# Experts' loop with rounds of 16 pairs on TensorE and of eight on ScalarE, expert words loaded within the steps, and sixteen staging buffers for normalised blocks

## What is computed

```python
scores = sigmoid(x @ gate_w.T);  sc = scores + gate_bias
group_scores = top_k(sc.reshape(T, 8, 8), 2)[0].sum(-1)     # 4 of 8 groups stay
tidx = top_k(masked, 8)[1]
tw = take_along_axis(scores, tidx) / sum * 2.5
y[t] = sum over the 8 experts e of tw * (silu(x We_gate[e]) * (x We_up[e])) We_down[e]
     + (silu(x Ws_gate) * (x Ws_up)) Ws_down
```

## Time and profile before

| | us |
|---|---|
| runs | median 1569.08 (1569.03 to 1569.74, three runs) |
| the profiled execution | 1555.25 |
| its span | 1553.5 |
| TensorE busy in the span | 1330.9 (86%) |
| VectorE busy | 933.4 (60%) |
| ScalarE busy | 850.4 (55%) |
| POOL busy | 626.7 (40%) |

### The profile page before, as it was taken

How to read it: one execution, slowest core, us unless ns; L and a number is a source line. 1 busy time by engine, 2 the same in 40 slices (tenths; PEclk the granted TensorE clock), 3 DMA queues, 4 the chain that set the end, 5 groups by cost and what they waited for, 6 DMA issues and landing times.

```text
span 1553.5 us, 38499 instructions
## 1 busy us (share of the span) xinstructions
PE 1330.9 (86%) x9262; PEld 1181.9 (76%) x9263; DVE 933.4 (60%) x4527; ACT 850.4 (55%) x2382; POOL 626.7 (40%) x750
## 2 busy tenths in 40 slices
PE   5873878788787897988888898988899789999996
PEld 5863767677666786877777777777787789999995
DVE  6771434334334453666666565665644589888997
ACT  2442565565555585554545454454555467777774
POOL 7026555556555500555555555655555300000000
PEclk9986788788898797999999999999999989999998
DMA  7034443532222200566666666666544443333322
GB/s 243 32 126 147 143 160 125 171 132 94 92 93 86 86 7 30 175 186 187 193 189 195 182 185 189 190 186 187 168 151 143 171 153 96 117 109 103 122 91 75
DMA packets 152813, 214.06 MB, mean 138 GB/s; under 512 B 25268, under 2 KB 125365, under 8 KB 148149
## 3 DMA queue, kind: packets, MB, share of 16 engines
q1 hardware_dynamic: 80450, 86.77, 17.7%
q0 software_dynamic: 28800, 82.20, 14.1%
q10 hardware_dynamic: 43520, 44.57, 11.3%
HBM read 113.86 MB, written 103.81 MB: 140 GB/s over the span
## 4 chain that ended last, share of the span: by engine, by line
PE 60%; DVE 12%; issue 11%; ACT 6%; another core or an unknown queue 5%; ACTq 2%; SPq 1%; DVEq 1%; DMA 1%
PE psS L982 19%; PE psO L991 5%; PE psM L991 4%; DVE x_all L1656 4%; PE psT L862 4%; PE psT L966 3%; PE psS L847 3%; PE psV L819 3%; PE psV L790 2%; PE psS L832 2%; ACT pr L1147 2%; PE psQ L752 2%; PE psT L876 2%; PE psQ L800 1%
## 5 line engine op out<-in xcount | busy, mean ns | idle before, releaser
L982 PEld LDWEIGHTS psS<-sm,wt 128*128 128x128 f32 x2560 | 304.2, 192 | 56.1 <-issue 50.3
L982 PE MATMUL psS<-sm,wt 128*128 128x128 f32 x2560 | 320.8, 278 | 16.7 <-ACT wt L1261 7.4
L641 POOL DMA_INDIRECT slot_rows<-x_out_st,idx_st x256 | 247.8, 968 | 175.0 <-issue 58.4
L669 POOL DMA_INDIRECT home_rows<-qz,row_idx x160 | 154.6, 966 | 207.3 <-DVE qz L1690 177.5
L1147 ACT ACTIVATE pr<-sm,nmax 128x192 f32<-128x192 f32 x512 | 205.5, 451 | 51.5 <-DVE nmax L1585 49.9
L1249 ACT ACTIVATE prT<-psS 128x256 f32<-128x256 f32 x160 | 61.9, 387 | 286.2 <-PE psS L982 182.6
L669 POOL DMA_INDIRECT home_rows<-sm,row_idx x160 | 154.4, 965 | 141.9 <-DVE sm L1690 99.7
L1155 ACT COPY prT<-psT 128x384 f32<-128x384 f32 x256 | 122.1, 477 | 149.3 <-PE psT L862 83.9
L1683 DVE TENSOR_TENSOR prT<-psS,prT 128x256 f32<-128x256 f32 x160 | 67.7, 423 | 203.8 <-ACT prT L1249 165.9
L1261 ACT COPY wt<-shared_mem 128x512 f32 x320 | 184.4, 633 | 4.8 <-issue 4.8
L862 PE MATMUL psT<-ident,pr 128*128 128x128 f32 x768 | 142.0, 297 | 49.4 <-ACT prT L1155 43.8
(11 more groups left out here) (290 smaller groups left out, 2725.6 us busy)
## 6 DMA issues: line engine op xcount, KB each, us to landing
shared_mem<-home_rows SPq DMA_DIRECT2D x32, 1024.0 KB, 5.1
pr<-slot_rows ACTq DMA_DIRECT2D x120, 272.0 KB
qz<-slot_rows ACTq DMA_DIRECT2D x40, 272.0 KB
slot_rows<-wt SPq DMA_DIRECT2D x32, 272.0 KB
shared_mem<-in_L_ffn_We_gate SPq DMA_DIRECT2D x64, 128.0 KB
shared_mem<-in_L_ffn_We_up SPq DMA_DIRECT2D x64, 128.0 KB
shared_mem<-in_L_ffn_We_down SPq DMA_DIRECT2D x64, 128.0 KB
x_all<-in_L_attn_x SPq DMA_DIRECT2D x4, 1024.0 KB, 9.6
```

Of the source, the lines that this page charges most:

```text
L641: pool.indirect_dma_start(slot_rows, bass.IndirectOffsetOnAxis(ap=idx_st[:, j, k:k + 1], axis=0), x_out_st[:, j % 2, :], None).then_inc(sc ...
L669: pool.indirect_dma_start(home_rows, bass.IndirectOffsetOnAxis(ap=row_idx[:, j, a:a + 1], axis=0), ys[j][:, a, :], None).then_inc(y_out[j] ...
L982: last = mm(psS[:, j % 2, (2 * a + n) * P:(2 * a + n + 1) * P], wt[j % 2][:, a, c, n * F:(n + 1) * F], xsT[:, j % 2, a, c, :], start=(c == ...
```

## The change

Three things are changed, and the arithmetic in none of them.

TensorE's rounds are of 16 pairs: first and last written out, a loop of eight rounds between them. ScalarE no longer loads four words at the start of a round of four. It loads the word of a pair at the end of the step before the one that copies its weights, and its loop has rounds of eight pairs, with a round of four written out before and after. The staging buffers of normalised blocks are sixteen: eight in `sm_mem`, as before, and eight in the memory of `qz`, which is not yet in use at that time.

```diff
@@ constants @@
-PE_ROUND = 8
+PE_ROUND = 16
+ACT_ROUND = 8
...
-XN = 8
+XN = 16
@@ buffers @@
-        xn_st = sm_mem[:].rearrange("p (j d) -> p j d", j=XN)
+        xn_st = [m.rearrange("p (j d) -> p j d", d=D)[:, n, :] for m in (sm_mem[:], qz[:].rearrange("p c u h t -> p (c u h t)"))
+                 for n in range(XN // 2)]
@@ SP @@
-                sp.dma_start(xn_tiles[i], xn_st[:, i % XN, :]).then_inc(xn_out[i % XN], 16)
+                sp.dma_start(xn_tiles[i], xn_st[i % XN]).then_inc(xn_out[i % XN], 16)
@@ TensorE, turn_x @@
-                                                   xn_st[:, (2 * m + n) % XN, c * P:(c + 1) * P], ident[:])
+                                                   xn_st[(2 * m + n) % XN][:, c * P:(c + 1) * P], ident[:])
@@ ScalarE @@
-            def step(j, g, nth, named, final=False):
-                u = g * XS + j
-                silu(j, u, nth < 2)
-                if not (final and j >= XS - 2):
-                    keep_tiles((j + 2) % XS, u + 2, False)
-                    keep_weights((j + 2) % XS, u + 2, named[j], False)
-                if not final:
-                    act.wait_ge(row_meta, u + 1)
-                    load_pair(j, u + XS)
+            def round_of(base, steps, first=False, final=False):
+                named = experts_of(base + 2)
+                for n in range(steps):
+                    u = base + n
+                    j = n % XS
+                    silu(j, u, first and n < 2)
+                    if not (final and n >= XS - 2):
+                        keep_tiles((j + 2) % XS, u + 2, False)
+                        keep_weights((j + 2) % XS, u + 2, named, False)
+                    if not final:
+                        act.wait_ge(row_meta, u + 1)
+                        load_pair(j, u + XS)
+                    if n < (steps - 3 if final else steps - 1):
+                        named = experts_of(u + 3)
...
-                named = [experts_of(j + 2) for j in range(XS)]
-                for j in range(XS):
-                    step(j, 0, j, named)
-                with act.Fori(1, PAIRS // XS - 1) as g:
-                    named = [experts_of(g * XS + j + 2) for j in range(XS)]
-                    for j in range(XS):
-                        step(j, g, MANY, named)
-                named = [experts_of(PAIRS - XS + j + 2) for j in range(XS - 2)]
-                for j in range(XS):
-                    step(j, PAIRS // XS - 1, MANY, named, final=True)
+                round_of(0, XS, first=True)
+                with act.Fori(0, (PAIRS - 2 * XS) // ACT_ROUND) as g:
+                    round_of(g * ACT_ROUND + XS, ACT_ROUND)
+                round_of(PAIRS - XS, XS, final=True)
@@ VectorE, normalise @@
-                    v.tensor_scalar(xn_st[:, i % XN, :], x_all[:, i, :], mean[:, i:i + 1], rstd[:, i:i + 1],
+                    v.tensor_scalar(xn_st[i % XN], x_all[:, i, :], mean[:, i:i + 1], rstd[:, i:i + 1],
```

## The result

The changed kernel takes 1582.56 us in the median (1574.23 to 1601.52, 11 runs), the kernel before 1569.08 (1562.07 to 1575.53, 11 runs): ratio 1.0083 with a 95% interval of 1.0062 to 1.0103. It is slower. The ratio is of runs at the usual granted clock; the one of 1601.52 us had a lower clock (0.81 for 0.92) and is left out of it. The profiled execution has a span of 1584.2 us.

A forecast was written before the change was run, and what follows sets the result against it. Bound: TensorE's signals held while POOL issues indirect DMAs in the experts' loop. Terms -32.4 - 5.3 - 1.3 - 3.0 = -42.0 against 1555.25 gave 1513.3, or 1527 us with the 13.83 offset; range 1482 to 1593.

The forecast's parts named there:

- What bounds the kernel: Experts' loop: while POOL issues several indirect DMAs without pause, TensorE's signals are held until about 1 us after the last.
- Words within the steps: ScalarE in the experts' loop: a single load fits beside a step's copies, removing thirty-odd pauses of 2.12 us.
- the 63.7 us: ScalarE's idle in 30 waits the profile doesn't explain, read as word loads; the gain was forecast as not that much.
- the 0.87 per cycle: TensorE's loss in us per four pairs that follows ScalarE's load pause; the other 1.87 was put down to a hold.
- What is late next: Experts' loop: without the pause, POOL's TENSOR_TENSOR makes a pair only 0.3 us late; 48 pairs at 3.12 us give -32.4 us.
- the stream: Experts' loop at the fast pace, POOL's DMAs in twos; forecast to last until the end of the second stretch, 48 pairs.
- the pause at 634.84: ScalarE's load pause, idle 2.16 us, taken to make one pair late and so end the loop's fast pace.
- Slower: the pauses kept POOL's runs apart: Rival, experts' loop: without pauses every run is four DMAs, 8.07 us per two pairs; +24, 1593 us; chance 0.18.
- the 13.83 us between it and the median: Profiled execution's 1555.25 us lay this far under the median 1569.08; the same distance was assumed for the forecast time.
- 3.63 us at the end of the loop: Pace per pair from two POOL runs, 7.26 us apart, cited against the slower rival.
- Rounds of 16: TensorE in the experts' loop: two words and a branch 9 times, not 19; five turnovers saved in the held stretch, -1.3 us.
- Sixteen staging blocks: Front, before routing: blocks 8 to 15 need no wait for stores, TensorE's idle goes; -3.0 us, between -1.5 and -7.

The follow-up runs named there:

- gap_after: Changed kernel plus POOL clearing 128 x 512 unread numbers after each pair's two homeward DMAs, which the next pair's DMAs wait for: 1532.39 us, ratio 0.977.
- gap256_after: Changed kernel plus POOL clearing 128 x 256 unread numbers after each pair's two homeward DMAs, with a wait for it: 1495.46 us, ratio 0.963.
- gap32_after2: Changed kernel plus POOL clearing 128 x 32 unread numbers after each pair's two homeward DMAs, with a wait for it: 1490.53 us, ratio 0.950.
- set 4: Fourth set of kernels run beside the kernel before on one chip, where signals are held; the kernel before took 1568.9 us.
- before_again: The kernel before, unchanged, run again for a second trace: 1569.23 us, ratio 1.000.
- pe16_only: Kernel before with only TensorE's rounds of 16 pairs: 1564.12 us, ratio 0.999.
- xn16_only: Kernel before with only the sixteen staging buffers: 1561.67 us, ratio 0.996.

## Why the prediction was wrong

- *What bounds the kernel*: right where signals are held. TensorE's signals are late while POOL issues; gap_after, gap256_after and gap32_after2, which only add a clearing and a wait to the changed kernel, are 2 to 5% faster than the kernel before, where the changed kernel is 0.8% slower.
- *Words within the steps*: right that a single load fits beside the copies (idle 0.38 for 2.12) and that the 63.7 us wouldn't be won. Even the 0.87 per cycle didn't come.
- *What is late next*: **this step failed**. "2.5 + 0.9 = 3.4 against 3.09, made up by the next pair's slack of 0.5. So I let the stream go on." I counted POOL's time alone and took any gap between runs of two for enough. The runs show in its place that signals are late with runs of two as well: in the changed kernel the silu at 637.90 comes 1.28 us after its gate-up ended, with 0.87 us between the runs. A stream of 3.09 a pair has no slack for that, and nothing in it forces POOL to keep two pairs apart: the next pair's DMAs began after 2.34 us of idle, and the two pairs behind them merged. It did not end because of the pause at 634.84 either, as I read the earlier trace rows: the changed kernel has no pause there, and its first run of four has the same place. Why the first signals come in time in both isn't shown. At 0.98 us of forced gap a pair takes 3.40, at 1.17 POOL's own 3.38; no run here keeps 3.09 through the loop where signals are held.
- *Slower: the pauses kept POOL's runs apart*: this is what happened. I had +28.4 us for the loop and a time of 1593; the runs have +17.8 (605.8 to 623.6, set 4) and 1582.56. The price of a merged run was right (8.07 against 8.08 and 8.13). Most merge, if not every one as I had it: 64 runs of four and 27 of two for 160 pairs, where before has 43 of four. What was off is the base: the trace that I worked from had a loop of 596.6 us where before_again, pe16_only and xn16_only have 605 to 607. It was a lucky execution, and so the 13.83 us between it and the median, which I carried over as a constant, was in part the loop itself (596.6 against 605.8). So this rival's 1593 is near the measured time with a part of its sum too large, and I gave it 0.18. The evidence that I weighed against this rival, 3.63 us at the end of the loop, comes from where VectorE has less to do per pair and POOL no TENSOR_TENSOR.
- *Rounds of 16*: -1.3 us expected, -2.0 measured with an interval of -5.5 to +1.6. The longer loop isn't fetched at each turn; the DMA queues of after over the same stretch as the earlier trace rows:

```profile
q8 instruction: 5, 0.08, 0.1%
q14 instruction: 1, 0.01, 0.0%
```

The five packets of q8 all lie before 760 us, in the first turn or two; from there to 1190 it has none, and q14 its one. By the rule of the Trainium skill that I weighed ("Runtime: NRT & Kernel Launch", section "Instruction fetch mechanics", the window of two pages) each turn of the loop should have fetched; the trace disagrees. The same section gives TensorE 128 KiB for instructions, which I passed over; sixteen pairs would fit into that, and the trace agrees with it.
- *Sixteen staging blocks*: -3.0 us expected (-7 to -1.5), -6.4 measured (-10.2 to -2.7). In the changed kernel TensorE goes straight into block 8:

```profile
22.06 1.81 PE L709 MATMUL psS<-gateT,xT_all 128*128 128x64 f32 x8
23.66 0.97 PE L701 MATMUL psT<-ident,qz 128*128 128x128 f32 x4
24.46 1.00 PE L709 MATMUL psS<-gateT,xT_all 128*128 128x64 f32 x8
```

Its four matmuls start at 23.66 with no idle, 3.1 us earlier than at 26.77. The rest is the case at the far end of my range: without the pause eight gate matmuls take 1.00 us from 24.46 on, before that 1.81; in the kernel before they take 1.81 up to those at 32.59 and 1.06 at 35.04. The windows show a granted clock of 1.00 on both sides of these changes, so they don't tell what they are. Routing is done 5.3 us earlier (42.57 for 47.91).

## What to carry to other kernels

A pause on one engine can be what keeps another engine's work apart. Before taking it away, ask what then runs without a gap, and whether anyone needs that gap; an idle that the profile puts down to an engine that had long finished is the place to look. And where a program's DMAs are issued by POOL, look at the space between them: here a microsecond of it per pair, bought with more work for POOL, was worth 5% over the kernel before (the staging buffers' 0.4% is in it). And run the kernel before in every set: the same file took 1308 or 1569 us. The kernel with the changed parts and this gap, gap32_after2, beats both kernels where signals are held (0.950), and costs 0.3% where they aren't.

## What was unexpected of the hardware

Signals of TensorE come late while POOL issues indirect DMAs. In the rows shown they came 0.6 to 0.7 us after a run of two had ended (639.27 in the changed kernel, 705.03 in gap256_after), 1.0 after a run of four (721.99, after 720.95), and 3.8 after the long series in attention (150.07, after 146.25). Gaps of 0.87 to 1.17 us between runs of two don't prevent it. What in the chip holds them is open. That was in three of five sets of runs. In the other two it was not seen in the loop, with the same instructions and the same durations on POOL, and the kernel before ran in 1308 us instead of 1556 to 1569.
